# Norm chain and expert choice in small steps, expert weights in 30 transfers, third batch's input behind the first S pass

## The reference

```python
x = x + tanh(g_xattn[0]) * L0_xattn(layernorm(x), ctx, ctx)        # att0: 16 heads of 8, 512 keys
x = x + tanh(g_ffn[0]) * L0_ffn(layernorm(x))                      # moe0: best 1 of 8 experts, hidden 512
# L1_xattn, inside the gate g_xattn[1], on z = layernorm(x):
#   y1 = ln(z + mha(z, z, z)); y2 = ln(y1 + mha(y1, ctx, ctx))      # att1: 256 keys; att2: 512 keys
#   h = relu(y2 @ fc1 + fc1_b) @ fc2 + fc2_b                       # the dense layer "f"
#   x3 = x + tanh(g_xattn[1]) * ln(y2 + h)
# L1_ffn, inside g_ffn[1], on z4 = layernorm(x3):
#   u = z4 + attention(rmsnorm(z4, g1))    # att3: causal, rotary, 4 key/value heads
#   out = x3 + tanh(g_ffn[1]) * (u + moe(rmsnorm(u, g2)))          # moe1: best 2 of 4 experts, hidden 384
#   moe: probs = softmax(xf @ gate); w, idx = top_k(probs, 2); w = w / sum(w); comb = onehot(idx) weighted by w
```

## Time and profile before

| | us |
|---|---|
| median of three executions | 1510.77 |
| profiled execution, its own time | 1513.04 |
| its span in the trace | 1511.2 |
| TensorE matmul busy | 1327.0 (88%) |
| VectorE busy | 891.8 (59%) |
| ScalarE busy | 694.5 (46%) |
| GpSimd busy | 304.9 (20%) |

### The profile page before, as it was taken

The page is one execution under the profiler, slowest core; times in us unless marked ns, Lnnn a source line. Parts: engine busy times, 40 slices in busy tenths (PEclk is TensorE's granted clock), DMA queues, the critical chain, the costliest instruction groups (busy, mean ns, idle before and its releaser), DMA issues.

```text
span 1511.2 us, 25307 instructions
## 1 busy us (share of the span) xinstructions
PE 1327.0 (88%) x8424; PEld 652.9 (43%) x8424; DVE 891.8 (59%) x1922; ACT 694.5 (46%) x1064; POOL 304.9 (20%) x896
## 2 busy tenths in 40 slices
PE   2799999979999997998889997978978779879998
PEld 1244444434444443444334443434445456544443
DVE  1568888733444444667568867768565767633433
ACT  1256666633334332656447654634434334323433
POOL 3222332100001001333223322312132323100000
PEclk9999999989999997889669998988879899869999
DMA  7344545310001301445554443523324334211110
GB/s 183 97 140 140 157 128 152 101 46 0 15 21 53 87 21 37 142 130 162 164 158 128 144 141 92 172 73 96 99 65 133 99 99 122 75 43 35 28 28 14
DMA packets 160727, 144.40 MB, mean 96 GB/s; under 512 B 11467, under 2 KB 135123, under 8 KB 160595
## 3 DMA queue, kind: packets, MB, share of 16 engines
q1 hardware_dynamic: 160598, 142.79, 32.5%
HBM read 79.05 MB, written 62.91 MB: 94 GB/s over the span
## 4 chain that ended last, share of the span: by engine, by line
issue 67%; POOLq 22%; PE 9%; DVE 1%; DMA 0%; ACT 0%; POOL 0%; DVEq 0%; SPq 0%; PEldq 0%
POOLq L848 5%; POOLq L821 4%; PE e_ps L1542 3%; PE av_ps L1553 3%; PE e_ps L1543 3%; POOLq L818 3%; POOLq L823 2%; POOLq L856 2%; POOLq L858 2%; POOLq L860 2%; PE misc L1534 1%; POOLq L836 1%; POOLq L867 1%; POOLq L876 0%; POOLq L863 0%
## 5 line engine op out<-in xcount | busy, mean ns | idle before, releaser
L908 ACT ACTIVATE prob<-e_ps 128x1024 f32<-128x1024 f32 (+1 forms) x384 | 379.0, 988 | 305.7 <-PE e_ps L1373 219.2
L1072 DVE TENSOR_REDUCE nmax<-s_ps 128x1 f32<-128x512 f32 x512 | 338.7, 687 | 110.3 <-PE s_ps L1339 108.9
L1373 PE MATMUL e_ps<-Qst,Kst 75*128 75x256 bf16 x1408 | 251.0, 293 | 27.6 <-DMA Qst<-mrow 20.9
L1391 PE MATMUL av_ps<-prob,Vx 128*32 128x256 f32 (+1 forms) x3072 | 261.5, 412 | 8.8 <-ACT FB L981 6.4
L1339 PE MATMUL s_ps<-Kst,Qst 72*128 72x512 bf16 x512 | 212.0, 416 | 47.0 <-DVE nmax L1072 42.0
L1076 DVE TENSOR_REDUCE nmax<-s_ps 128x2 f32<-128x512 f32 x256 | 173.6, 688 | 129.3 <-PE s_ps L1345 65.2
L1373 PEld LDWEIGHTS e_ps<-Qst,Kst 75*128 75x128 bf16 x1408 | 140.6, 104 | 94.8 <-issue 24.9
L1191 DVE TENSOR_TENSOR prob<-prob,s_ps 128x512 f32<-128x512 f32 x128 | 87.8, 686 | 147.7 <-ACT prob L958 147.0
L958 ACT ACTIVATE prob<-e_ps,b 128x512 f32<-128x512 f32 x128 | 87.9, 687 | 147.6 <-PE e_ps L1472 146.2
L1345 PE MATMUL s_ps<-Kst,Qst 72*128 72x256 bf16 x512 | 128.9, 307 | 19.5 <-DVE nmax L1076 19.2
L1472 PE MATMUL e_ps<-FB,wbig 128*128 128x512 f32 x256 | 137.4, 628 | 0.0
(11 more groups left out here) (179 smaller groups left out, 1633.7 us busy)
## 6 DMA issues: line engine op xcount, KB each, us to landing
q_parts<-qp SPq DMA_DIRECT2D x96, 192.0 KB, 2.4
k_parts<-kp SPq DMA_DIRECT2D x48, 384.0 KB, 3.9
Qst<-q_parts SPq DMA_DIRECT2D x128, 144.0 KB
Kst<-k_parts SPq DMA_DIRECT2D x64, 288.0 KB
k_parts<-kp SPq DMA_DIRECT2D x48, 192.0 KB, 2.4
Kst<-k_parts SPq DMA_DIRECT2D x64, 144.0 KB
ctxT<-in_ctxT SPq DMA_DIRECT2D x16, 256.0 KB, 4.9
wbig<-in_w SPq DMA_DIRECT2D x8, 512.0 KB, 5.5
```

The lines of the kernel that those rows point to most:

```text
L908: act.activation(dst, src, ACT.Exp).then_inc(e_drained, 1)
L1072: ve.tensor_reduce(nmax[:, g, u, h % GH:h % GH + 1], s_ps[:, u, :], AX.X, ALU.max, negate=True).then_inc(s_drained, 1)
L1373: last = pe.matmul(o, Ks[0:KROWS, par, h, t * P:t * P + P], Qst[0:KROWS, par, h, :], start=True, stop=not a.rope)
L1391: last = pe.matmul(av_ps[VW * hh:VW * hh + VW, SQ - w:SQ], Vx[:, par, t, h, :], prob[:, place, off * SQ:off * SQ + w], start=(t == 0), sto ...
```

## The change

What it does:

- `f.back`, `f.t2`, `f.t3`, `f.t4` become `f.back`, `f.stat` (three times), `f.norm`, `f.gain`, `f.shift`, `f.gate`, `f.again`, `f.rms`, `f.gain1`, at places 13, 14, 15 and 0, 1, 2, 3, 5, 6, 8, 10 of the next body; `f.nT` goes from 9 to 11, the three stores to 4, 7 and 12. The same instructions are issued.
- `m1.choose` becomes five steps at places 9 to 13 (in moe1: k = 8 to 12). The same instructions are issued.
- The weights come one expert and one matrix at a time at places 4 and 12: 16 transfers of 256 KB in bodies 0 to 7, two of 256 KB in body 8 (both at place 4), 12 of 192 KB in bodies 9 to 14. That is 30 transfers, and the semaphore totals follow.
- At the start, `xstat` of batch 2 goes behind the S pass; `maxT` 0, the stores of batch 1 and `loadin` of batch 2 go behind the fifth slot of the pass, in this order.

```diff
 # ffn_items
-        put(n, 14, ("f.back", i, None))
-        put(n, 15, ("f.t2", i, None))
-        put(n + 1, 1, ("f.store", i, 0))
-        put(n + 1, 2, ("f.t3", i, None))
-        put(n + 1, 5, ("f.t4", i, None), ("f.store", i, 1))
-        put(n + 1, 9, ("f.nT", i, None))
-        put(n + 1, 10, ("f.store", i, 2))
+        put(n, 13, ("f.back", i, None))
+        put(n, 14, ("f.stat", i, 0))
+        put(n, 15, ("f.norm", i, None))
+        put(n + 1, 0, ("f.gain", i, None))
+        put(n + 1, 1, ("f.shift", i, None))
+        put(n + 1, 2, ("f.gate", i, None))
+        put(n + 1, 3, ("f.stat", i, 1))
+        put(n + 1, 4, ("f.store", i, 0))
+        put(n + 1, 5, ("f.again", i, None))
+        put(n + 1, 6, ("f.stat", i, 2))
+        put(n + 1, 7, ("f.store", i, 1))
+        put(n + 1, 8, ("f.rms", i, None))
+        put(n + 1, 10, ("f.gain1", i, None))
+        put(n + 1, 11, ("f.nT", i, None))
+        put(n + 1, 12, ("f.store", i, 2))
 ...
-        put(n, 9, ("m1.choose", i, None))
+        for k in range(5):
+            put(n, 9 + k, ("m1.choose", i, k))
 # body
-    if n < 2 * B and n % B in (0, 5, 6, 7):
-        put(7, ("weights", n, None))
+    for k in range(2):
+        if n < 2 * B and not (n == B and k == 1):
+            put((4, 12)[k], ("weights", n, k))
 # start_steps
-    out += [("loadx", 2, None), ("xstat", 2, None), ("loadin", 2, None)]
-    for n, s in plan[None]:
+    out += [("loadx", 2, None)]
+    for k, (n, s) in enumerate(plan[None]):
         for u in range(2):
             out += s_units(n, s, u)
-    return out + [("qstore", 1, None), ("kstore", 1, None), ("maxT", 0, 0)]
+        if k == att(0).gs:
+            out += [("maxT", 0, 0), ("qstore", 1, None), ("kstore", 1, None), ("loadin", 2, None)]
+    return out + [("xstat", 2, None)]
 # SyncE, kind == "weights"
-                        q = {0: 0, 5: 1, 6: 2, 7: 3}[b]
-                        ex = slice(q * E0 // 4, (q + 1) * E0 // 4)
-                        sp.dma_start(w1_0[:, ex, :], dram["w1_0"][:, ex, :]).then_inc(w0_loaded, 16)
-                        sp.dma_start(w2_0[:, ex, :, :], dram["w2_0"][:, ex, :, :]).then_inc(w0_loaded, 16)
+                        if arg == 0:
+                            sp.dma_start(w1_0[:, b, :], dram["w1_0"][:, b, :]).then_inc(w0_loaded, 16)
+                        else:
+                            sp.dma_start(w2_0[:, b, :, :], dram["w2_0"][:, b, :, :]).then_inc(w0_loaded, 16)
 ...
-                        dst, src = {5: (w1_1, "w1_1"), 6: (w3_1, "w3_1"), 7: (w2_1, "w2_1")}[b]
-                        sp.dma_start(dst, dram[src]).then_inc(w1_loaded, 16)
+                        k = 2 * (b - 1) + arg
+                        if k < 3 * E1:
+                            dst, src = ((w1_1, "w1_1"), (w3_1, "w3_1"), (w2_1, "w2_1"))[k // E1]
+                            sp.dma_start(dst[:, k % E1], dram[src][:, k % E1]).then_inc(w1_loaded, 16)
 # VectorE, ffn_step: f.t2 is cut where its drains stood (f.t3 and f.t4 likewise)
-                elif kind == "f.t2":
+                elif kind == "f.stat":
+                    stats_of(LF, f_res2 if arg == 1 else f_res, BT).then_inc(f_stats, 1)
+                elif kind == "f.norm":
                     ve.wait_ge(f_rstd, f_stat("f", n, 0))
                     apply_norm(LF, f_res, f_res, BT)
+                elif kind == "f.gain":
                     ve.drain()
                     ve.tensor_tensor(f_res, f_res, over("ffn_g", BT), ALU.mult)
+                elif kind == "f.shift":
                     ve.drain()
                     ve.tensor_tensor(f_res, f_res, over("ffn_b", BT), ALU.add)
+                elif kind == "f.gate":
 ...
```

More of the change, by code:

```diff
@@ L331, in moe1_steps @@
             put(7, ("m1.gate", 3, None))
-            put(8, ("m1.choose", 3, None))
+            for k in range(5):
+                put(8 + k, ("m1.choose", 3, k))
         for e in range(2, E1):
@@ L628, in program @@
         LATE = 16 * 9
-        W0 = 16 * 8
-        W1 = 16 * 5
+        W0 = 16 * 2 * E0
+        W1 = 16 * (2 + 3 * E1)
         def f_stat(kind, i, s):
@@ L873, in step @@
                     rsqrt(LF, BT, False).then_inc(f_rstd, 1)
-                elif kind in ("f.back", "f.t2", "f.t3"):
-                    s = ("f.back", "f.t2", "f.t3").index(kind)
+                elif kind == "f.stat":
                     po.drain()
-                    po.wait_ge(f_stats, f_stat("f", n, s))
-                    rsqrt(LF, BT, s == 2).then_inc(f_rstd, 1)
+                    po.wait_ge(f_stats, f_stat("f", n, arg))
+                    rsqrt(LF, BT, arg == 2).then_inc(f_rstd, 1)
             for st in STEPS:
@@ L987, in step @@
                     act.activation(fT, misc[:, :], ACT.Copy).then_inc(misc_drained, 1)
-                elif kind == "m1.choose":
+                elif kind == "m1.choose" and arg == 0:
                     act.wait_ge(exp_in, n + 1)
@@ L1055, in step @@
                 elif kind[0:2] == "f.":
-                    ffn_step(kind, n)
+                    ffn_step(kind, n, arg)
                 elif kind[0:3] == "m1.":
@@ L1206, in moe0_step, with ffn_step @@
                     apply_norm(LF, m0_norm, m0_new, BT).then_inc(m0_normed, 1)
-            def ffn_step(kind, n):
+            def ffn_step(kind, n, arg):
                 if kind == "f.back":
@@ L1224, in ffn_step @@
                                             op1=ALU.add)
-                    stats_of(LF, f_res2, BT).then_inc(f_stats, 1)
-                elif kind == "f.t3":
+                elif kind == "f.again":
                     ve.wait_ge(f_rstd, f_stat("f", n, 1))
                     apply_norm(LF, f_res, f_res2, BT)
-                    stats_of(LF, f_res, BT).then_inc(f_stats, 1)
-                elif kind == "f.t4":
+                elif kind == "f.rms":
                     ve.wait_ge(f_rstd, f_stat("f", n, 2))
                     apply_norm(LF, f_out, f_res, BT, rms=True)
+                elif kind == "f.gain1":
                     ve.drain()
@@ L1250, in moe1_step @@
                     ve.drain()
-                    ve.tensor_reduce(mx[:, :], l, AX.X, ALU.max)
-                    ve.drain()
-                    ve.tensor_tensor(l2, l, wide(mx), ALU.subtract).then_inc(exp_in, 1)
-                    ve.wait_ge(exp_out, n + 1)
-                    ve.tensor_reduce(mx[:, :], l3, AX.X, ALU.add)
-                    ve.drain()
-                    ve.reciprocal(mn[:, :], mx[:, :])
-                    ve.drain()
-                    ve.tensor_tensor(l, l3, wide(mn), ALU.mult)
@@ L1260, in moe1_step @@
-                    ve.drain()
-                    one_hot(oh1[:, :, 0:E1], l, E1, mx)
-                    ve.scalar_tensor_tensor(out=l2, in0=oh1[:, :, 0:E1], scalar=-2.0, in1=l, op0=ALU.mult, op1=ALU.add)
-                    ve.drain()
-                    one_hot(l3, l2, E1, mx)
-                    ve.tensor_tensor(l2, oh1[:, :, 0:E1], l3, ALU.add)
-                    ve.drain()
-                    ve.tensor_tensor(l3, l2, l, ALU.mult)
-                    ve.drain()
-                    ve.tensor_reduce(mx[:, :], l3, AX.X, ALU.add)
@@ L1270, in moe1_step @@
-                    ve.drain()
-                    ve.reciprocal(mn[:, :], mx[:, :])
-                    ve.drain()
-                    ve.tensor_tensor(comb[:, n, :, :], l3, wide(mn), ALU.mult).then_inc(m1_chosen, 1)
+                    if arg == 0:
+                        ve.tensor_reduce(mx[:, :], l, AX.X, ALU.max)
+                        ve.drain()
+                        ve.tensor_tensor(l2, l, wide(mx), ALU.subtract).then_inc(exp_in, 1)
+                    elif arg == 1:
+                        ve.wait_ge(exp_out, n + 1)
+                        ve.tensor_reduce(mx[:, :], l3, AX.X, ALU.add)
+                        ve.drain()
+                        ve.reciprocal(mn[:, :], mx[:, :])
+                        ve.drain()
+                        ve.tensor_tensor(l, l3, wide(mn), ALU.mult)
+                    elif arg == 2:
+                        one_hot(oh1[:, :, 0:E1], l, E1, mx)
+                    elif arg == 3:
+                        ve.scalar_tensor_tensor(out=l2, in0=oh1[:, :, 0:E1], scalar=-2.0, in1=l, op0=ALU.mult,
+                                                op1=ALU.add)
+                        ve.drain()
+                        one_hot(l3, l2, E1, mx)
+                    else:
+                        ve.tensor_tensor(l2, oh1[:, :, 0:E1], l3, ALU.add)
+                        ve.drain()
+                        ve.tensor_tensor(l3, l2, l, ALU.mult)
+                        ve.drain()
+                        ve.tensor_reduce(mx[:, :], l3, AX.X, ALU.add)
+                        ve.drain()
+                        ve.reciprocal(mn[:, :], mx[:, :])
+                        ve.drain()
+                        ve.tensor_tensor(comb[:, n, :, :], l3, wide(mn), ALU.mult).then_inc(m1_chosen, 1)
```

2 lines of the change are left out of this document (1 added, 1 removed).

## The result

| | us |
|---|---|
| the changed kernel, median of 16 executions (lowest to highest) | 1506.04 (1484.84 to 1527.84) |
| the kernel before, beside it, 16 executions | 1513.45 (1509.38 to 1533.87) |
| ratio, 95% interval | 0.988 (0.985 to 0.991) |
| forecast, range | 1466, 1440 to 1492 |

A forecast was written before the change was run, and what follows sets the result against it. TensorE, busy 88% of the span, was taken as the bound, so gains come from its standstills and slow clock. 9.1 + 21.0 + 8.9 + 5.9 = 44.9 off 1510.77 gave 1466 us, range 1440 to 1492.

The forecast's parts named there:

- C: Choice of experts in att3, split into steps: 8.9 us less, bounds 3 and 17.
- D: Weights in smaller transfers during att0 and att1: 5.9 us less, bounds -5 (loss) and 12.
- A: Start, with `xstat` behind the S pass and the first `maxT` in it: 9.1 us less, bounds 5 and 10.
- B: Dense layer's norm chain in att2, in small steps: 21.0 us less, bounds 8 and 46.
- two thirds of wait and clock: Windows 24 and 26: 2/3 x (12.1 + 0.34 x 28.8) = 14.6 us returned, less 3 for what is late next: 11.6.
- `v` and `proj` no longer stand behind the chain: Att3: 6.5 us of the 4.9 and 3.2 us waits return, plus 2.4 of clock: 8.9.
- rival 2: VectorE is the limit and spreading only moves the wait: B returns 8, C 4, total 1486 us; chance 0.18.
- a quarter of the bytes is 0.6, ... I take 2.0: Bodies 9 to 14: 12 transfers of 192 KB delay rows 0.6 us each, 7.2 at most; 2.0 us taken as cost.
- the waits go, but for 1.2: Att1: TensorE's row waits of 2.34 and 3.6 us behind large weight transfers go but for 1.2, returning 4.7 us.
- rival 3: Weights in front of rows in bodies 9 to 14 delay them and the clock falls: 45 us more, 1517; chance 0.04.
- The price: Low clock, from windows 11 and 12 doing the same work: 0.34 us lost per us at the low level.
- rival 1: The clock comes back too, as fewer standstills leave TensorE at 2.4 GHz: 25 us more gained, 1441; chance 0.20.

The follow-up runs named there:

- norm_only: The kernel before with only the dense layer's norm chain in small steps; ratio 0.9882, -17.9 us.
- choice_only: The kernel before with only the choice of experts in five steps at places 9 to 13; ratio 1.0004, +0.6 us.
- weights_only: The kernel before with only the weights in 30 transfers; ratio 1.0020, +3.0 us.
- sn_late_weights: The kernel before with the change's start and norm chain, and moe1's weights in 12 transfers in att2 instead of att1; ratio 0.9767.
- sn_all: sn_late_weights plus the choice split two and three over two bodies, batch 17's context and input later, `f.h` at places 7 and 8; 0.9643, 1458.0 us.

## Why the prediction was wrong

Of the 26.7 us that were missing, C and D account for 18.4 (14.8 less predicted, 3.6 more measured), and A and B, each measured alone, for 5.7.

**A, start: right.** The waits named went, the times of the first maximum and the first E came within half a us, and the first rows of batch 1 come 9.9 us sooner in the mean of the profiles. 6.5 (0 to 13) for 9.1: the size is within the measurement.

**B, norm chain: the waits went as said, and the failed step is "two thirds of wait and clock".** Windows 20 and 22 at VectorE's own pace were the best step of the prediction. The size, 17.9 for 21.0 in norm_only, seems luck in part: start and chain together gave 16, not the 24.4 of the two alone, and windows 19 to 26 are only 8 us shorter in the mean of seven profiles. I had taken every low stretch to lie at a long wait for a maximum. In the trace of before, of 79 low us in windows 19 to 26 only 37.5 begin during such a wait (2.8 us and more) or within 3 us behind it; the other 41 begin elsewhere, and my term took these as returned all the same. What I missed besides is what is late next. I looked for it on VectorE and at the transposes of `f.back`; it is `f.h` at place 5, whose input comes up to 1.7 to 2.8 us late, and the E and AV behind it (1.2 to 1.84 us). They stood in the trace of before among larger waits, and my term said nothing of them. With them in place, the low clock of windows 19 to 26 came back in three of seven profiles (38 to 51 low us) and not in four (65 to 102).

**C, choice: the failed step is "`v` and `proj` no longer stand behind the chain", worth 8.9; measured nothing (+0.6, between -6.7 and +7.9).** It is true of these two. But between places 9 and 15 VectorE also has `v`, `proj`, statistics and `apply`; it was busy 8.41 of the 11 us from 1231.5 to 1242.5 in choice_only, beside drains, and what it owed came out at the next user, `normed`. I had written that down as rival 2 and priced it at 4 us returned. With three of the steps in the next body's first places, where VectorE waits 2.6 us for S units between 1244 and 1251 us of the trace of before, windows 27 to 30 are 5.8 us shorter in the mean than with all five at 9 to 13, and the ratios of the two forms, 0.991 and 1.000, have intervals that just part.

**D, weights: the failed step is "a quarter of the bytes is 0.6, ... I take 2.0", and "the waits go, but for 1.2"; 5.9 less predicted, 3.0 more measured.** One wait moved: with the weights gone from place 7, the rows of place 13 of body 14 wait 2.7 to 3.5 us behind k's stores, an input and a context (four profiles), 2.4 us even with no weights. I had looked for the waits that would go and not for the transfers that the old wait had given time. And rows held up by 0.6 to 1.5 us cost little by themselves, but in windows 10 to 12 they fell in with another short wait, and the clock fell; my 2.0 had no clock in it. This is rival 3's mechanism, at a quarter of its price (45): windows 10 to 12 of weights_only take 24.4, 23.5 and 22.4 us, those of sn_late_weights 19.5, 20.2 and 19.0, 11.6 us less.

**The clock.** The price was about right: within the executions of one kernel time rises by 0.39 us per low us (all kernels' executions together), and I took 0.34. But I tied the clock to the long waits. It falls as well, though not each time, behind one of 1.2 to 1.9 us, or two of 0.5 us and more close together, and the change turned few long waits into many short ones: from 60 us on TensorE's pauses of 1.2 us and more went from 27 with 70 us to 32 with 63. In the fastest form but one (sn_all) 19 with 39 us are left, and the low us of its executions are 173 in the mean, against 251 for the kernel before in the first two sets and 258 for the full change. So rival 1 came true, as far as these runs show, of a kernel that removes these pauses, and not of this change.

**The chances.** The sign was right; the median, 1506, lies 14 us above the range, since I gave rivals 2 and 3 as alternatives of the whole, while each held for one part.

## What to carry to other kernels

- When a long wait goes, list every wait above a us in that stretch of the trace of before: these are what is left, and the clock can fall behind them as well. Moving `f.h` by two places was worth more than each of three of the change's four parts.
- Spreading a chain only helps into places where its engine idles: look at that engine's busy time from the chain to the end of what it owes, not at the length of a step. A window boundary can hide that a wait moved; sum both sides, and over more than one profile.
- A bulk transfer belongs in a stage whose small urgent transfers have slack, not in smaller pieces in front of them.
